# Attention sums of a four-layer graph network: TensorE's product three items behind the spread of the maxima, VectorE's addition four behind

## The reference

```python
score = attn_score * (relation_pri[etype] / SQRT_DK)
m = jax.ops.segment_max(score, col_idx, num_segments=n)
ex = jnp.exp(score - m[col_idx])
denom = jax.ops.segment_sum(ex, col_idx, num_segments=n)
alpha = ex / denom[col_idx]
agg = jax.ops.segment_sum(alpha[..., None] * msg_edge, col_idx, num_segments=n)
```

## Time and profile before

| | |
|---|---|
| time, median of 3 runs | 4121.35 us (4117.49 to 4123.58) |
| profiled execution, its own time | 4122.4 us |
| its span | 4120.6 us |
| mean granted TensorE clock | 0.848 |
| TensorE matmul busy in the span | 3136.8 us, 76% |
| TensorE weight loads | 2152.0 us, 52% |
| VectorE | 2230.6 us, 54% |
| ScalarE | 892.4 us, 22% |
| GpSimd | 2742.2 us, 67% |

### The profile page before, as it was taken

How to read it: one execution, slowest core, us unless ns; L and a number is a source line. 1 busy time by engine, 2 the same in 40 slices (tenths; PEclk the granted TensorE clock), 3 DMA queues, 4 the chain that set the end, 5 groups by cost and what they waited for, 6 DMA issues and landing times. The chain is left out here.

```text
span 4120.6 us, 64202 instructions
## 1 busy us (share of the span) xinstructions
PE 3136.8 (76%) x11666; PEld 2152.0 (52%) x11666; DVE 2230.6 (54%) x7572; ACT 892.4 (22%) x2584; POOL 2742.2 (67%) x2879
## 2 busy tenths in 40 slices
PE   5999938787788775796888877888886776676663
PEld 2444416665566653343767766677544444444442
DVE  8300027666666655445788868677654343434435
ACT  1333300000200000341444456555210000100000
POOL 3777767777677776335777767777127777477774
PEclk9999959989889986898787779777888887778876
DMA  4333323333333334677555546555123333333332
GB/s 142 146 144 143 144 78 106 106 105 105 96 106 105 105 106 133 242 292 247 163 166 163 165 139 175 161 163 162 41 62 105 105 106 105 99 105 105 106 105 90
DMA packets 226896, 540.00 MB, mean 131 GB/s; under 512 B 73482, under 2 KB 107948, under 8 KB 212876
## 3 DMA queue, kind: packets, MB, share of 16 engines
q0 software_dynamic: 136528, 374.97, 30.7%
q1 hardware_dynamic: 57880, 103.46, 6.9%
q10 hardware_dynamic: 32164, 57.91, 4.8%
HBM read 390.04 MB, written 146.09 MB: 130 GB/s over the span
## 5 line engine op out<-in xcount | busy, mean ns | idle before, releaser
L604 POOL DMA_INDIRECT gcn_edges_g<-table,rows_i x782 | 740.6, 947 | 430.8 <-ACTq L875 193.2
L923 PE MATMUL ps<-gcn_edges_g,gcn_edges_onehot 128*128 x1760 | 626.7, 498 | 313.0 <-SPq L620 277.8
L969 DVE TENSOR_TENSOR acc<-acc,ps 128x256 f32 (+1 forms) x880 | 370.0, 420 | 745.0 <-PE ps L923 733.0
L923 PEld LDWEIGHTS ps<-gcn_edges_g,gcn_edges_onehot 128*128 128x128 f32 x1760 | 392.9, 242 | 536.8 <-issue 483.4
L307 POOL DMA_INDIRECT records<-rec,slots x391 | 375.9, 961 | 184.3 <-issue 124.2
L604 POOL DMA_INDIRECT score_g<-table8v,rows_i x391 | 379.3, 970 | 132.5 <-issue 112.4
L604 POOL DMA_INDIRECT rel_g<-table,rows_i x391 | 372.1, 952 | 135.1 <-issue 95.4
L604 POOL DMA_INDIRECT score_g<-table8k,rows_i x391 | 371.4, 950 | 128.7 <-issue 112.1
L604 POOL DMA_INDIRECT conv_edges_g<-table,rows_i x391 | 370.8, 948 | 127.4 <-issue 94.5
L359 PE MATMUL ps<-w,xt 128*128 128x512 f32 x1000 | 435.8, 595 | 18.3 <-ACT xt L329 18.3
L1048 PE MATMUL ps<-q,onehot_t 128*128 x880 | 320.9, 500 | 107.2 <-DVE onehot_t L1147 84.3
(11 more groups left out here) (319 smaller groups left out, 4762.3 us busy)
## 6 DMA issues: line engine op xcount, KB each, us to landing
table<-tb SPq DMA_DIRECT2D x50, 1280.0 KB, 4.6
score_dst_bc<-dst_rows ACTq DMA_DIRECT2D x110, 256.0 KB, 3.5
sum_dst_bc<-dst_rows ACTq DMA_DIRECT2D x110, 256.0 KB, 3.5
gcn_edges_g<-table,rows_i POOLq DMA_INDIRECT x782, 2.8
table<-gcn_tb SPq DMA_DIRECT2D x50, 128.0 KB, 1.7
records<-rec,slots POOLq DMA_INDIRECT x391
rel_g<-table,rows_i POOLq DMA_INDIRECT x391, 2.9
conv_edges_g<-table,rows_i POOLq DMA_INDIRECT x391, 2.8
```

What stands on the lines that cost most here:

```text
L604: pool.indirect_dma_start(out=m.g[:, 2 * slot_of(p) + j, 0:D], out_offset=None, in_=table, in_offset=bass.IndirectOffsetOnAxis(ap=m.rows_i ...
L923: mm = pe.matmul(bank(m, i % BANKS, 0, width), m.onehot[:, 2 * k + j, :], window(m.g, slot + j, 0, width), start=(j == 0), stop=(j == 1))
L969: nc.vector.tensor_tensor(acc, acc, bank(m, i % BANKS, 0, width), ALU.add).then_inc(added, 1)
```

## The change

TensorE's pass i now holds the spread of item i and the product of item i-3; VectorE's pass i ends with the addition of item i-4. Both loops run one pass longer. All counts that are waited for by an item are the same as before for that item; no buffer is added.

```diff
@@ def tensor(pe):
-        for i in range(ITEMS + 2):
+        for i in range(ITEMS + 3):
...
             regs.load(i + 1)
-            if i >= 2:
-                kk = (i - 2) % UNROLL
-                pe.wait_ge(onehot_ready, i - 1)
-                pe.wait_ge(by_dve, i - 1)
-                pe.wait_ge(by_act, i - 1)
-                pe.wait_ge(added, i - 1)
+            if i >= 3:
+                kk = (i - 3) % UNROLL
+                pe.wait_ge(onehot_ready, i - 2)
+                pe.wait_ge(by_dve, i - 2)
+                pe.wait_ge(by_act, i - 2)
+                pe.wait_ge(added, i - 2)
...
@@ def vector(dve):
-        for i in range(ITEMS + 3):
+        for i in range(ITEMS + 4):
...
-            if i >= 3:
-                add(i - 3)
+            if i >= 4:
+                add(i - 4)
```

## The result

The changed kernel takes 4246.9 us (median of 6 runs, 4243.63 to 4253.13), the kernel before 4119.6 us beside it. The ratio is 1.031, with a 95% interval of 1.030 to 1.032. The forecast was no change, 4121.5.

What follows compares the result with a forecast made beforehand. GpSimd's gathers were taken to bound the stage. Resumption +0.6, later releases 0 and the end -0.5 summed to +0.1 us on the profiled 4122.4; from the runs' median of 4121.35 this gave 4121.5 us, range 4117 to 4129.

Steps and rivals of the forecast that it cites:

- What bounds the kernel before: Stage from 2434 to 2911 us: GpSimd's gathers set its length; the other engines are faster and run out of edges.
- Added slack: TensorE's product and VectorE's addition one pass later: most of 59.7 us of product waits go, worth nothing beside the gathers.
- A wait that gets tighter: VectorE's second mask waits for item i-4's product, now behind the previous spread: 1.88 or 2.60 us an item, costing nothing.
- from O to the next T 1.36: On VectorE, from an item's second mask to the next item's first mask: 1.36 us, at either clock.
- Is that still faster than GpSimd: Items at 2.16 us against 2.28 that GpSimd allows; some 14 us of cover left, so no cost.
- rival 1: Second mask's wait (L1327): items become the bound above 2.25 us each; +12 us, 4134, at 70% lower clock; chance 0.09.
- the thing corrects itself: Argument against items becoming the bound: the clock fell behind empty rings, which get rarer when items are slower.
- The chip's clock: TensorE busy 77 of 100 us, between two stretches that held 1.00; clock does not reach the time while GpSimd is last.
- The resumption: Stage's start: the product of item 1, and so GpSimd's resuming, comes 0.6 us later; bounds 0 and 1.07.
- Later releases: Ring pairs released one pass later, some 1.9 us; taken as 0, bounds 0 to 5 us.
- The end: Behind the last arrival, the last product follows without its 0.5 us gap: -0.5 us, bounds -1 to +3.
- The gathers themselves: GpSimd's gathers keep their times, 0.946 us median and 0.965 mean: no change.

Runs made afterwards that it cites:

- five masks: Five buffers in place of four for the masks of the sums, against the changed kernel: 4120.8 us, beside 4121.0 of the kernel before.
- load between: VectorE's register load put between the two masks, ahead of the wait for the product, against the changed kernel: 4119.2 us, beside 4121.1 of the kernel before.
- kernel with 256 more columns: One more TensorE matmul of 256 columns per item behind the product, result unused, against the changed kernel: 4157.3 us.
- filler kernel: One more TensorE matmul of 8 columns per item behind the product, result unused, against the changed kernel: 4304.7 us.
- kernel before with the tighter wait: Masks of the sums wait for the product of item i-3, not i-4, against the kernel before: 5700.0 us against 5526.6, on a chip with slow transfers.
- load first: VectorE's register load put ahead of both masks, against the changed kernel: 4207.3 us.

## Why the prediction was wrong, point by point

- **What bounds the kernel before:** right. With the loop out of the way (five masks, load between) the stage is again as long as the gathers, 4119 to 4121 us.
- **Added slack:** right. The addition's waits fell from 59.7 to 1.9 us and brought nothing.
- **A wait that gets tighter:** the loop was found and is the cause, but its term "from O to the next T 1.36" was taken from a pass in which O did not wait. Behind a wait VectorE's queue has lost its lead, and the register load between O and D comes to light: 1.84. The other part was 3.64, not 3.85: from the product's weights to O 2.14, where 2.15 + 0.15 had been added up, and 1.02 for 1.07 ahead of it. In sum 2.74 us an item at the lower clock, not 2.60, 0.20 above TensorE's own 2.54 and not 0.06.
- **Is that still faster than GpSimd:** here the forecast broke. "At the clock shares of now" took 46% at the lower level as given. They were 94% (0.53). With these, and 2.29 for the upper level as the kernel with 256 more columns showed it (not 1.88), 0.94/2.74 + 0.06/2.29 is 0.369 items per us, 2.71 us an item, where 2.72 was measured. With the shares of now and these loops it would have been 0.46/2.74 + 0.54/2.29 = 0.404, 2.48 us, which is already slower than the 2.25 from which rival 1 decides. So by this estimate the mis-sized loop alone would have turned the sign, by 151 x 0.23 = 35 us, and the clock made it 127.
- **Rival 1** named the mechanism and had 0.09. Its price used 70% as the far end, and its counter-argument ("the thing corrects itself") was false: full rings do not bring the clock up. I had read the low clock of the second stretch as a consequence of empty rings. The filler kernel and the changed kernel have full rings, and clocks of 0.50 and 0.53.
- **The chip's clock:** I weighed 77 of 100 us of busy time against two stretches at 1.00. Busy time in the records is no measure for this: 100% busy went with 0.50, and 85% with 1.00. Even the 71% that went with 1.00 in the earlier trace rows went with 0.50 in the kernel before with the tighter wait. What moves the clock is open.
- **The resumption:** right. T(0) came 1.9 us later in this run and GpSimd resumed at 2446.61; from T(0) that is 10.49 us, before 9.90, so 0.6 more.
- **Later releases:** taken as 0 because by 2447.5 a product took 1.11 us. In the changed kernel the one at 2447.12 took 2.07, and GpSimd's first further wait, 0.82 us, came at 2452.12. It is the same error, a clock carried over.
- **The end:** beside the point once the items were the bound.
- **The gathers themselves:** right, median 946 ns as before.

## What to carry to other kernels

Moving a consumer later in one engine's order moves every reuse of its buffers later too: count, for each ring, how many passes lie between the release and the next write, on the waiting engine as well, and give the ring one buffer more before the product goes one pass later. When a new wait appears on an engine, price what follows it from a pass in which that engine had just waited, not from an undisturbed one: here O to the next T, with the same register load in it, took 1.36 us in the one and 1.84 in the other, and 1.14 with the load moved away. And never carry TensorE's clock shares over to a changed pace; work both levels out and ask what the stage does if it stays at the lower.

## What the runs showed of the hardware

TensorE's granted clock did not follow its busy time in the records. From 2460 on, with a product of 260 columns each 3.01 us and small matmuls filling the rest, it was busy 100% at 0.50; with a product each 2.72 us, 96% and 0.53; with the load first, 2.51 us on average ((2993.7 - 2443.8) / 219 for its additions), 90% and 0.67; with 256 more columns in each item of 2.29 us, 85% and 1.00. The same share occurs at both levels: 14.29 of 20 us at 1.00, and 71.51 of 100 us (3648 to 3748) at 0.50 in the kernel before with the tighter wait. What the clock goes by is not settled by these; neither gaps nor busy time in the records tell it.

```profile
L1355 DVE TENSOR_TENSOR acc<-acc,ps x220: 409/416/426, 2443.8 to 2993.7; 128x260 f32 x110
```

The Trainium skill (TensorE: Matmul & The Clock Gate, section "HAM oscillation — how this bites in real kernels") has idle gaps as what closes the gate. It speaks of waits for a DMA between groups of matmuls, and not of a short gap in each item, to which my prediction stretched it. No run here contradicts it, but it does not cover the kernel with 8 more columns: there the clock was at 0.50 when the stage began, behind 16 us of idle, and it stayed there for the 540 us in which the records show no gap.

A register load on VectorE (from a table in memory) was measured in three places of its order. Between O and D it costs nothing where O did not wait, and about 0.4 us where O did: O to D is 0.43 us with it where O did not wait, 0.86 where it did, and 0.40 to 0.45 with the load moved. D to W is 0.30 us with the load ahead of D and 0.07 with it moved, so it may cost another 0.2 us there. In all, O to the next T is 1.84, 1.54 and 1.14 us with the load behind O, ahead of T and beneath O's wait. The profile put the time ahead of D down to the semaphore that came last, the spread's (72.8 us), which had nothing to do with it.
